# A hybrid layer (mixer, experts, attention, experts): weight slots refilled per half, a counter of its own for the decay requests, and the attention's heads written out

## The reference, cut to what matters

```
x = x + mixer(layernorm(x))        # 1024 tokens x 512, 128 heads of 64, 8 groups
x = x + experts(layernorm(x))
x = x + attention(layernorm(x))    # 32 heads of 16, causal, plus 10 adapter tokens
x = x + experts(layernorm(x))

mixer:  proj = x @ in_proj_w.T     # gate | hidden, B, C | dt
        hBC = silu(conv4(proj[hBC]) + conv_b)      # causal, per channel
        A_dt = dt * A;  A_cum = cumsum(A_dt) in chunks of 128 tokens
        Y_diag = C . B^T * exp(A_cum[l] - A_cum[s]) applied to hidden * dt
        Y_off  = C . previous state * exp(A_cum)
        y = Y_diag + Y_off + hidden * D
        out = rmsnorm_per_group(y * silu(gate)) * norm_w @ out_proj_w.T
```

## Time and the profile before

| | |
|---|---|
| median of 3 runs | 3026.96 us (3026.04 to 3036.11) |
| profiled execution, its own time | 3024.93 us |
| its span, first to last instruction | 3023.0 us |
| busy in the span | PE 91%, DVE 70%, ACT about a third, POOL about a quarter |
| mixer | about the first 2150 us of the span |
| attention's heads | 2490 to 2830 us of the span |

### The profile page before, as it was taken

How to read it: one execution, slowest core, us unless ns; L and a number is a source line. 1 busy time by engine, 2 the same in 40 slices (tenths; PEclk the granted TensorE clock), 3 DMA queues, 4 the chain that set the end, 5 groups by cost and what they waited for, 6 DMA issues and landing times. The chain is left out here.

```text
span 3023.0 us, 44437 instructions
## 1 busy us (share of the span) xinstructions
PE 2765.2 (91%) x15936; PEld 1813.1 (60%) x15936; DVE 2107.6 (70%) x3247; ACT 1018.3 (34%) x2081; POOL 734.8 (24%) x576
## 2 busy tenths in 40 slices
PE   3699999999999999999999999999699989888899
PEld 2366666666665666666666666567487454444388
DVE  5587787778777777867877877786554646666364
ACT  1233233333232233333332333323211326666421
POOL 1232242232323323222322432223221001111031
PEclk7899999999999999999999999999898989999999
DMA  4101121220211111112011211201201411111000
GB/s 161 27 16 40 28 73 30 39 71 15 49 47 45 45 30 65 24 51 69 20 40 28 73 32 43 65 17 25 78 0 73 146 43 38 36 36 37 1 11 18
DMA packets 117024, 134.71 MB, mean 45 GB/s; under 512 B 28065, under 2 KB 88561, under 8 KB 114161
## 3 DMA queue, kind: packets, MB, share of 16 engines
q1 hardware_dynamic: 111392, 130.37, 15.2%
q10 hardware_dynamic: 5456, 2.00, 0.3%
HBM read 113.96 MB, written 18.38 MB: 44 GB/s over the span
## 5 line engine op out<-in xcount | busy, mean ns | idle before, releaser
L452 PE MATMUL bank<-xnT,wh 128*128 128x512 f32 x1280 | 578.0, 603 | 50.9 <-issue 26.2
L546 PE MATMUL bank<-xnT,wg 128*128 128x128 f32 x4096 | 480.2, 275 | 0.0
L546 PEld LDWEIGHTS bank<-xnT,wg 128*128 128x128 f32 x4096 | 467.5, 192 | 3.3 <-issue 3.3
L589 PE MATMUL bank<-wo,yt 128*128 128x512 f32 x1024 | 455.3, 598 | 5.8 <-DVE yt L840 5.8
L735 DVE SCALAR_TENSOR_TENSOR cacc<-raw,cwh,cacc 128x512 f32<-128x512 f32 x480 | 439.7, 916 | 17.0
L452 PEld LDWEIGHTS bank<-xnT,wh 128*128 128x128 f32 x1280 | 237.7, 192 | 324.7 <-issue 290.1
L589 PEld LDWEIGHTS bank<-wo,yt 128*128 128x128 f32 x1024 | 194.7, 192 | 246.1 <-issue 246.0
L938 POOL TENSOR_TENSOR rr<-rr,nhalf 128x1 f32<-128x1 f32 x64 | 35.2, 549 | 959.2 <-DVE rr L873 959.2
L732 DVE TENSOR_SCALAR cacc<-raw,cwh 128x512 f32<-128x512 f32 x160 | 147.5, 922 | 134.6 <-ACT raw L720 133.9
L642 ACT ACTIVATE cth<-cacc 128x512 f32<-128x512 f32 x160 | 101.4, 634 | 405.4 <-DVE cacc L735 405.2
L1974 DVE TENSOR_REDUCE at_nm<-bank 128x1 f32<-128x512 f32 (+3 forms) x256 | 148.0, 588 | 110.4 <-PE bank L1840 91.7
(11 more groups left out here) (242 smaller groups left out, 4429.7 us busy)
## 6 DMA issues: line engine op xcount, KB each, us to landing
EC<-ecum_scratch SPq DMA_DIRECT2D x112, 256.0 KB
wh<-w_hs_dram SPq DMA_DIRECT2D x80, 256.0 KB, 10.4
wg<-w_gate_dram SPq DMA_DIRECT2D x8, 2048.0 KB, 7.5
wo<-w_out_dram SPq DMA_DIRECT2D x8, 2048.0 KB, 8.8
qk_scratch<-at_part SPq DMA_DIRECT2D x48, 256.0 KB
at_qT<-qk_scratch SPq DMA_DIRECT2D x32, 192.0 KB, 2.6
at_kT<-qk_scratch SPq DMA_DIRECT2D x32, 192.0 KB, 2.6
wgu<-w_gu_dram SPq DMA_DIRECT2D x1, 3584.0 KB, 11.6
```

The lines of the kernel that those rows point to most:

```text
L452: mm = nc.tensor.matmul(BA[bank][:, :], wh[:, j, k, :], xnT[:, k, h * HALF:(h + 1) * HALF], start=(k == 0), stop=(k == KC - 1))
L546: mm = nc.tensor.matmul(BA[b][:, i * P:(i + 1) * P], wg[:, k, j * P:(j + 1) * P], xnT[:, k, ttok], start=(k == 0), stop=(k == KC - 1))
L589: mm = nc.tensor.matmul(BA[b][:, :], yt[:, j * P:(j + 1) * P], wo[:, j, :], start=(j == 0), stop=(j == JT - 1))
```

## The change

`wh` has five slots instead of ten. Tile i of any half goes to slot i mod 5, with one semaphore for each slot, and SP refills a slot with the tile that comes five places later as soon as the one in it has been used, in both halves of a group. SP's order in the mixer is now by slots: the requests of `next_rows`, then the refills for this slot's tiles. The decay requests count on a semaphore of their own, `d_ec`, for which DVE waits; PE's differences wait for `d_rw` alone, and the rows of the next slot are asked for before the wait for DVE's use of `EC`. The heads of the attention, and SP's loads for them, are written out with constants.

```diff
-        wh = sb(ctx, "wh", [P, PT, KC, P])
+        wh = sb(ctx, "wh", [P, WR, KC, P])          # WR = PT // 2 = 5
...
-            pe.wait_ge(d_wh[j], 16 * p[0] + 16)
+            pe.wait_ge(d_wh[i % WR], 16 * (2 * step + i // WR + 1))
...
             if quarters[0] == 0:
-                pe.wait_ge(d_rw, 32 * 15 * g + 64 * z + 32)
+                pe.wait_ge(d_rw, 32 * n + 32)
...
             if z > 0:
-                dve.wait_ge(d_rw, 32 * 15 * g + 64 * z + 32)
+                dve.wait_ge(d_ec, 32 * skip_last(g, z, 1))
...
                 def next_rows(g, z):
                     pe_df.wait(sp, 4 * (8 * g + z + 1))
                     sp.sem_inc(turned, 1)
-                    if z > 0:
-                        dv_yo.wait(sp, skip_first(g, z, 2) + 2)
                     if z < NT - 1:
                         load_rows(g, z + 1)
+                        if z > 0:
+                            dv_yo.wait(sp, skip_first(g, z, 2) + 2)
+                            sp.sem_inc(turned, 1)
                         load_decay(g, z + 1)
                     else:
                         load_rows(g + 1, 0)
...
+                def next_tile(p, i):
+                    if p[1] is None:
+                        return
+                    last = isinstance(p[0], int) and p == (G - 1, 1)
+                    if i >= WR and last:
+                        return
+                    pe_P.wait(sp, (2 * p[0] + p[1]) * PT + i + 1)
+                    sp.sem_inc(turned, 1)
+                    load_tile(sp, p[0] + (p[1] if i >= WR else 0), (i + WR) % PT)
+
+                for i in range(PT):
+                    next_tile((0, 0), i)
+
+                def slot_loads(g, z, end):
+                    if not (end and z == NT - 1):
+                        next_rows(g, z)
+                    if z == 0 and not end:
+                        po_cw.wait(sp, 2 * g + 1)
+                        load_taps(g + 1, 0)
+                    step, mine = tiles_of(g, z)
+                    for i in mine:
+                        next_tile(step, i)
+                    if end:
+                        return
+                    if z == 3:
+                        po_cw.wait(sp, 2 * g + 2)
+                        load_taps(g + 1, 1)
+                    if z == 5:
+                        dv_out.wait(sp, 8 * g + CH)
+                        dv_st.wait(sp, skip_last(g, CH, 2))
+                        load_pack(g + 1, 0)
...
-                    for z in range(4):
-                        next_rows(g, z)
-                    po_cw.wait(sp, 2 * g + 1)
-                    load_taps(g + 1, 0)
-                    for i in range(PT):
-                        if i in (4, 7):
-                            next_rows(g, 4 if i == 4 else 5)
-                        pe_P.wait(sp, (2 * g + 1) * PT + i + 1)
-                        sp.sem_inc(turned, 1)
-                        load_tile(sp, g + 1, i)
-                    po_cw.wait(sp, 2 * g + 2)
-                    load_taps(g + 1, 1)
...
+                    for z in range(NT):
+                        slot_loads(g, z, False)
...
-                    for k in range(QS):
-                        body(k, k)
-                    with eng.Fori(0, AH // QS - 2) as i:
-                        for k in range(QS):
-                            body(QS * i + QS + k, k)
-                    for k in range(QS - 1):
-                        body(AH - QS + k, k)
+                    for h in range(AH - 1):
+                        body(h, h % QS)
                     last(AH - 1, QS - 1)
```

More of the change, by code:

```diff
@@ L149, in mixer @@
     with ExitStack() as ctx:
+        WR = PT // 2
         xnT = sb(ctx, "xnT", [P, KC, T])
         mask = sb(ctx, "mask", [P, P])
-        wh = sb(ctx, "wh", [P, PT, KC, P])
+        wh = sb(ctx, "wh", [P, WR, KC, P])
         wg = sb(ctx, "wg", [P, KC, GC])
         wo = sb(ctx, "wo", [P, JT, C])
-        d_wh = [sem(ctx, f"d_wh{j}") for j in range(PT)]
+        d_wh = [sem(ctx, f"d_wh{j}") for j in range(WR)]
         d_wg, wo_set = sem(ctx, "d_wg"), sem(ctx, "wo_set")
@@ L160, in load_tile @@
             j = ORDER[i]
-            sp.dma_start(wh[:, j, :, :], A["w_hs"][bass.ds(g, 1), :, j].rearrange("o p k m -> p (o k) m"))\
-                .then_inc(d_wh[j], 16)
+            sp.dma_start(wh[:, i % WR, :, :], A["w_hs"][bass.ds(g, 1), :, j].rearrange("o p k m -> p (o k) m"))\
+                .then_inc(d_wh[i % WR], 16)
         def load_gate(sp, g):
@@ L199, in _ @@
                             .then_inc(s_x[i], 16)
-                    for i in range(PT):
+                    for i in range(WR):
                         load_tile(sp, 0, i)
@@ L419, in mixer @@
         d_pk = [sem(ctx, f"d_pk{h}") for h in range(2)]
-        d_rw = sem(ctx, "d_rw")
+        d_rw, d_ec = sem(ctx, "d_rw"), sem(ctx, "d_ec")
         SHARE = [(0, 4), (4, 7), (7, 10), (10, 10)]
@@ L449, in pe_tile @@
             step = 2 * p[0] + h
-            pe.wait_ge(d_wh[j], 16 * p[0] + 16)
+            pe.wait_ge(d_wh[i % WR], 16 * (2 * step + i // WR + 1))
             for k in range(KC):
-                mm = nc.tensor.matmul(BA[bank][:, :], wh[:, j, k, :], xnT[:, k, h * HALF:(h + 1) * HALF],
+                mm = nc.tensor.matmul(BA[bank][:, :], wh[:, i % WR, k, :], xnT[:, k, h * HALF:(h + 1) * HALF],
                                       start=(k == 0), stop=(k == KC - 1))
@@ L972, in load_decay @@
                                      ecum_dram[bass.ds(g * HG, HG), z * P:(z + 1) * P].rearrange("(j s) t -> s j t", s=2)
-                                     [side:side + 1].broadcast_to([64, JT, P])).then_inc(d_rw, 16)
+                                     [side:side + 1].broadcast_to([64, JT, P])).then_inc(d_ec, 16)
                 def load_rows(g, z):
@@ L994, in next_rows @@
                         load_rows(g + 1, 0)
-                for g in range(G - 1):
-                    for z in range(4):
-                        next_rows(g, z)
-                    po_cw.wait(sp, 2 * g + 1)
-                    load_taps(g + 1, 0)
-                    for i in range(PT):
-                        if i in (4, 7):
-                            next_rows(g, 4 if i == 4 else 5)
-                        pe_P.wait(sp, (2 * g + 1) * PT + i + 1)
-                        sp.sem_inc(turned, 1)
-                        load_tile(sp, g + 1, i)
-                    po_cw.wait(sp, 2 * g + 2)
-                    load_taps(g + 1, 1)
[L1011 to L1015, removed]
+                def next_tile(p, i):
[27 more added lines that the diff above has]
+                        load_pack(g + 1, 0)
+                for g in range(G - 1):
+                    for z in range(NT):
+                        slot_loads(g, z, False)
                     pe_gt.wait(sp, 2 * (8 * g + 8))
@@ L1020, in _ @@
                     load_pack(g + 1, 1)
-                for z in range(NT - 1):
-                    next_rows(G - 1, z)
+                for z in range(NT):
+                    slot_loads(G - 1, z, True)
             @block.gpsimd
@@ L1767, in _ @@
                         load(k, k)
-                    with sp.Fori(0, AH // QS - 1) as i:
+                    for i in range(AH // QS - 1):
                         for k in range(QS):
```

## The result

The changed kernel takes **2985.96 us** (median of 4 runs, 2984.41 to 2986.53), the kernel before 3029.58 us in the same measurement (3026.04 to 3036.11). The ratio is 0.9853, with a 95% interval of 0.9834 to 0.9872. The forecast was 2986 us, faster. In the profiled executions the span fell by 40.3 us, from 3023.0 to 2982.6. The total was met closely; what it is made of was not quite what the forecast said, and the experiments show where.

What follows compares the result with a forecast made beforehand. PE, busy 91%, was taken as the bound, its longest wait being for the `EC` transfer. Terms of -36.3, 0 and -4.4 us summed to -40.7: 2984.2 us for the profiled execution, 2986 us median, range 2976 to 3005.

Steps and rivals of the forecast that it cites:

- Term 1: Mixer: a separate counter for decay requests leaves PE's differences waiting for rows alone, removing the `EC` waits; -36.3 us.
- a slot with four tiles and no wait lasts 35.88 us, so the floor is 249.73: Mixer: a group's unheld time, the seventh group's 250.78 us less 1.05 for its first slot's `EC` wait.
- a long idle time costs more than itself: Mixer: the slot at 1018.34 lost 2.42 us for a PE idle time of 2.00 us.
- The removed wait's place: PE: some removed idle time returns as waits for DVE at L833, total up from 22.1 to about 35 us.
- Term 2: Mixer weight tiles: five slots instead of ten, 80 more requests of 256 KB, refills covered by 36.8 us; cost 0.
- as now: Mixer: after the change `EC` is still asked for 1.3 us into a slot.
- Term 3: Attention: heads 4 to 27 written out take 10.60 us each instead of 10.78 in the loop; -4.4 us.
- more collisions: Rival: POOL's `wo` weighting holds DVE's L771 in more groups, 5.3 us each; six more give 3018 us; chance 0.05.
- the change does not touch what is ahead of `wo`: Mixer: whether `wo` lands just before or after L771 is chance of a few tenths of a microsecond, one in seven.
- Renamed wait: Rival: PE really waits for rows, or refills push them past 12 us of a slot; 3023 us; chance 0.04.
- Late refills: Rival: refills over 36.8 us make PE wait at L450; slower than 3042 us; chance 0.03.
- The loop gives nothing: Rival: writing out the attention's heads saves no time; 2991 us; chance 0.04.

Runs made afterwards that it cites:

- experiment 2: Kernel before, with only the decay requests (`EC`) counted on a semaphore of their own; ten weight slots and the loop stay: 3007.71 us, ratio 0.9925.
- experiment 10: Changed kernel with `wo` weighted on ACT in eight operations spread over the first slot, none on POOL: 2978.61 us, ratio 0.9811 to the kernel before.
- experiment 3: Changed kernel with the hardware loops put back for the attention's heads and SP's loads: 3006.89 us.
- experiment 5: Changed kernel with two weight slots instead of five: 2987.00 us.
- experiment 1: Changed kernel with rows and decay requests counted on one semaphore again, PE's differences waiting for both: 2999.35 us, ratio 0.99.
- experiment 4: Kernel before with only the attention's heads and SP's loads for them written out: 3013.35 us, ratio 0.9943.
- experiment 9: Changed kernel with the loops put back and POOL's weighting of `wo` made to wait for DVE's L772 of the same slot: 2995.23 us, ratio 0.9868.
- experiment 11: Changed kernel with the loops put back and one unused 1.6 MB input declared ahead of all others: 2993.39 us, ratio 0.987.
- experiment 7: Changed kernel with DVE waiting for `wo` and a small memset before L772 in each group's first slot, so POOL's weighting starts first: 3027.75 us.
- experiment 8: Changed kernel with the decay requests made three times, the first two copies into unused buffers, DVE waiting for all: 3357.08 us.

## Why the prediction was right, and where it was not

**Term 1, the counter (-36.3 us).** The mechanism held: all waits on `EC` are gone, DVE never waits for it, the other slots are at the floors read from before to 0.01 us, and experiment 2 shows that the counter alone is enough. The size was met, 34.1 us in the main stretch against 34.4, but by two errors that cancel, and that is luck. The step "a slot with four tiles and no wait lasts 35.88 us, so the floor is 249.73" took the first slot of a group to be like its fifth. It is not: POOL's weighting delays DVE there by several microseconds, which the `EC` wait used to hide, and the first slots of the later groups ended 0.8 to 1.5 us over it, 7.1 us in seven, 5.7 of them in the main stretch. Experiment 10 takes the weighting off POOL, and then 35.88 is indeed the floor. The other error is the 5.3 us that I left in for one collision; in the changed kernel's profile there was none. In the last group's first slot the gain was 0.5 us for 1.9, for the same reason.

The step "a long idle time costs more than itself" was right, and the trace shows why, which the forecast did not say. Behind the 2.00 us in the slot at 1018.34 the granted clock was at half (a window, read as in experiment 3):

```profile
1033.20:1036.60 3.40, 2.88 (x11) 1.71 (x12) 2.65 (x3) 3.40 (x7) 1.90 (x1) 0.50 0.13 47
```

In the main stretch of the kernel before there are five such places, 20.4 us at 1.2 GHz in all. In each the clock fell during an idle time of PE or up to 2.5 us behind it; other idle times of 1 to 2.4 us had no fall behind them. In the changed kernel's main stretch there is none. An estimate from this is that up to 10 of the 34.1 us came from the clock, not from the waits themselves.

**The removed wait's place.** I expected the total of L833 to grow from 22.1 to about 35 us. It became 23.4 (31 times). What appeared was the wait at L595, 5.2 us, behind DVE's reduction, which I had not named. It stands in the first slots alone and is gone in experiment 10, so it is not what a removed `EC` wait gives back in any slot, but part of the 7.1 us above. In the other slots nothing came back: they are at their floors.

**Term 2, the refills (0).** Right, with a cover far larger than needed: experiment 5 shows no cost with two slots. That SP's new order helps `EC` land was right too and worth more than I said: experiment 1 has 8 waits where the kernel before had 21, though a part of this is that `EC` is asked for some 0.6 us sooner, where I wrote "as now". The two edits overlap, so their gains don't add.

**Term 3, the heads (-4.4 us).** The trace gave 4.6, and experiments 3, 4 and 9 gave it again at either kind of code. But writing out the heads did more than term 3 says. In all three profiles with the loops and no guard or unused input, the one of before among them, L771 is held in one to three groups; in none of those with the heads written out, but for the forced one. Experiment 11 shows that an unused input, with no instruction changed, goes with later landings of `wo` and no collision, as the written-out heads do. So the heads seem to act on the mixer by where things lie in memory and hence when `wo` lands. That the layout is the way is shown for the unused input only, with one profile of each program; for the heads it is the explanation that fits, not one that was tried by itself. It shifts the odds and does not decide alone: experiments 2 and 3 each have one run of four that is 8 us below the others, and experiment 11 one that is 7 us above, and none of these has a profile.

**The rival "more collisions".** I gave it 0.05 and wrote that "the change does not touch what is ahead of `wo`" and that its landing is chance. It is not chance alone: it depends on the program's layout, and experiments 2 and 3 had three collisions each. The price of 5.3 us was about right: the slots with the collision in experiments 2 and 3 are 4.3 to 5.9 us over the 36.69 us of first slots without it, and in experiment 7 it is 6.0 us with the later start. With the heads left in the loop, the change would have come out near 3007 us, outside my range of 2976 to 3005, and the rest of the sum would have been no worse. That the change also wrote out the heads, for 4.6 us of their own, kept it in the range. The chance of this rival should have been several times larger.

**The other rivals.** Renamed wait: refuted, no wait on `RW` anywhere. Late refills: refuted by experiment 5. The loop gives nothing: refuted.

**What stays open.** The 3.5 us between the mixer and the heads that experiment 9 has over the changed kernel, and why the landing of `wo` is later in one layout than in another.

## What to carry to other kernels

A wait that counts two kinds of transfers on one semaphore costs the slower one; look in the list of waits for an engine that waits on a buffer it does not read. When the price of a wait is taken from slots without it, take slots of the very same kind, because the wait may be hiding another engine's lateness. And two products on DVE and POOL that start within some tenths of a microsecond of each other are a coin toss that a change of layout far away can turn: put an explicit order between them, or move one to an engine that holds nobody. And when a wait of TensorE is priced, look at the granted clock behind it.

## What the runs showed of the hardware

- DVE's product of two SBUF tiles took 7.8 to 8.1 us instead of 1.2 where a POOL operation of 7.02 us had started 0.02 to 0.34 us earlier (experiments 2, 3 and 7), while a memset passed in 0.11 us (experiment 7). Where DVE started 0.02 us earlier, it took 1.2 us and POOL 8.1. Products on ACT of the same data held nobody (experiment 10).
- TensorE's granted clock fell to 0.50, 1.2 GHz, for 3.4 or 6.8 us during or behind idle times of 3.4 to 3.7 us (the four slots with the collision in the kernel before and experiment 3). By the estimate above this was a third to a half of what the collision cost.
- A 256 KB weight tile fetched by itself landed in 2.5 us at the least and 2.7 at the median; several at a time took a median of 10.4.
- `EC`'s transfers, of the same size and shape in every group, are faster in two of the eight. In the changed kernel the median landing is 7.4 us in the third and the seventh group and 8.8 to 9.2 in the others, and none of the 15 `EC` waits of the kernel before in the slots 3 to 5 lies in these two. In experiment 8 the third group's slot from 782.60 to 816.03 is at its floor of 33.43 us, the fourth group's from 1048.21 to 1088.36 lasts 40.15, and the seventh group is like the third:

```profile
782.60 0.77 PE L521 MATMUL bank<-em,xch 128*64 128x128 f32 x10 [0.16 <-issue]
...
816.03 0.77 PE L521 MATMUL bank<-em,xch 128*64 128x128 f32 x10
...
1048.21 0.91 PE L521 MATMUL bank<-em,xch 128*64 128x128 f32 x6 [6.40 <-issue]
...
1088.36 0.91 PE L521 MATMUL bank<-em,xch 128*64 128x128 f32 x6 [5.18 <-issue]
```
